# Unit 0 put in another order, index lists fetched one at a time, and one of nine tables gathered instead of looked up in units 3, 5 and 7

## What is computed

```
e = stack([tbl_f[ids[:, f]] for f in range(26)], axis=1)        # 2048 x 26 x 128
combined = concatenate([dense[:, None, :], e], axis=1)          # 2048 x 27 x 128
inter = einsum('bfd,bgd->bfg', combined, combined)              # 27 x 27 for each sample
z = concatenate([dense, inter[:, iu0, iu1]], axis=1)            # 128 + 351
h = concatenate([z, dense], axis=1)                             # 607
h = maximum(h @ W_top1 + b_top1, 0)                             # 512
h = maximum(h @ W_top2 + b_top2, 0)                             # 256
y = h @ W_top3                                                  # 1
```

## Time and profile before

| | |
|---|---|
| median of 3 runs | 402.04 us (401.98 to 402.32) |
| the profiled execution: its time | 402.14 us |
| its span in the trace | 400.4 us |
| PE / PEld / DVE / ACT / POOL busy | 376.2 / 369.1 / 275.1 / 190.2 / 261.3 us |
| granted TensorE clock, mean | 0.991 of full speed |

### The profile page before, as it was taken

How to read it: one execution, slowest core, us unless ns; L and a number is a source line. 1 busy time by engine, 2 the same in 40 slices (tenths; PEclk the granted TensorE clock), 3 DMA queues, 4 the chain that set the end, 5 groups by cost and what they waited for, 6 DMA issues and landing times.

```text
span 400.4 us, 7798 instructions
## 1 busy us (share of the span) xinstructions
PE 376.2 (94%) x3136; PEld 369.1 (92%) x3136; DVE 275.1 (69%) x278; ACT 190.2 (48%) x427; POOL 261.3 (65%) x281
## 2 busy tenths in 40 slices
PE   1998599699999999999999999999999999999996
PEld 1887498599999999999999999999999999999996
DVE  5679582997878486866687486867687486862451
ACT  3475344436642465325642465326643465426643
POOL 7777465777777757776677757776677757774000
PEclk9999799999999999999999999999999999999999
DMA  6944522233324323322324233332323333321000
GB/s 244 383 135 112 186 76 63 52 104 79 87 59 101 81 72 88 79 82 70 90 54 109 74 79 87 80 80 71 90 60 101 78 80 79 81 55 39 2 2 1
DMA packets 18059, 35.49 MB, mean 89 GB/s; under 512 B 5628, under 2 KB 7292, under 8 KB 18024
## 3 DMA queue, kind: packets, MB, share of 16 engines
q0 software_dynamic: 8704, 17.84, 17.9%
q1 hardware_dynamic: 9224, 17.15, 14.2%
q10 hardware_dynamic: 96, 0.00, 0.0%
HBM read 34.97 MB, written 0.01 MB: 87 GB/s over the span
## 4 chain that ended last, share of the span: by engine, by line
PE 92%; DVE 3%; issue 1%; ACT 1%; DMA 1%; SPq 0%; DVEq 0%
PE l_ps L351 31%; PE g_ps L381 28%; PE t_ps L360 7%; PE l_ps L343 6%; PE h_ps L393 5%; PE h_ps L394 5%; PE h_ps L395 5%; PE h_ps L440 2%; PE t_ps L389 1%; DMA hot_idx<-in_hot_ids 1%; DVE onehot L569 1%; DVE zf L599 1%; ACT xT L720 1%; PE g_ps L393 0%; DVE zg L592 0%
## 5 line engine op out<-in xcount | busy, mean ns | idle before, releaser
L317 POOL DMA_INDIRECT emb<-in_tbl,idx x272 | 259.2, 953 | 104.7 <-issue 69.8
L569 DVE TENSOR_TENSOR onehot<-hot_idx,rows_ps 128x2048 fp32r<-128x2048 int32 x72 | 162.4, 2283 | 10.3 <-DMA hot_idx<-in_hot_ids 6.2
L381 PE MATMUL g_ps<-xT 128*123 128x108 f32 x1024 | 118.4, 273 | 5.5 <-DVE hot_low L579 4.7
L381 PEld LDWEIGHTS g_ps<-xT 128*123 128x123 f32 x1024 | 115.3, 190 | 6.0 <-issue 5.9
L351 PE MATMUL l_ps<-onehot,hot_low 128*128 128x256 f32 x528 | 76.5, 287 | 3.2 <-DVE onehot L569 1.8
L351 PE MATMUL l_ps<-onehot,hot_high 128*128 128x256 f32 x528 | 74.1, 283 | 0.0
L740 ACT COPY zg<-g_ps 27x216 f32<-27x216 f32 x160 | 52.8, 330 | 44.8 <-PE g_ps L381 43.7
L351 PEld LDWEIGHTS l_ps<-onehot,hot_low 128*128 128x128 f32 x528 | 67.5, 191 | 4.2 <-ACT xT L720 2.2
L351 PEld LDWEIGHTS l_ps<-onehot,hot_high 128*128 128x128 f32 x528 | 68.1, 192 | 0.0
L720 ACT COPY xT<-l_ps 128x512 f32<-128x512 f32 (+1 forms) x40 | 25.0, 624 | 80.2 <-PE l_ps L351 72.6
L592 DVE COPY zg<-g_ps 27x216 f32<-27x216 f32 x96 | 36.9, 384 | 34.6 <-PE g_ps L381 33.0
(11 more groups left out here) (64 smaller groups left out, 301.2 us busy)
## 6 DMA issues: line engine op xcount, KB each, us to landing
hot_idx<-in_hot_ids SPq DMA_DIRECT2D x36, 256.0 KB, 3.5
stage<-in_hot_tables SPq DMA_DIRECT2D x9, 512.0 KB, 10.2
emb<-in_tbl,idx POOLq DMA_INDIRECT x272, 2.7
dT<-in_dense_t SPq DMA_DIRECT2D x8, 128.0 KB, 2.1
wz<-in_W_pairs SPq DMA_DIRECT2D x1, 512.0 KB
w2s<-in_W_top SPq DMA_DIRECT2D x1, 512.0 KB, 6.6
wz<-in_W_dense SPq DMA_DIRECT2D x1, 256.0 KB
wd<-in_W_dense SPq DMA_DIRECT2D x1, 256.0 KB
```

Of the source, the lines that this page charges most:

```text
L317: pool.indirect_dma_start(emb[:, t % 2, n, :], None, tables[COLD[n]][:, :], bass.IndirectOffsetOnAxis(ap=idx[:, t, n:n + 1], axis=0)).then ...
L381: last = pe.matmul(g_ps[c % 2][0:TALL, i, 0:WIDE], four.rearrange("d s f -> d (s f)")[:, 0:TALL], four[:, :, 0:FEATS], start=True, stop=True)
L569: dve.tensor_tensor(onehot[n % ONEHOTS][:], here, rows, ALU.is_equal).then_inc(onehot_ready, 1)
```

## The change

Three things are changed.

- **Unit 0.** Only three tables (0, 1, 2) are looked up uncut, in place of six; tables 3 to 8 are cut first, in that order, and 0 to 2 last. The programs of PE, DVE and ACT for unit 0 are written in another order to go with it. `one_hot(1, 1)` and `one_hot(1, 2)` move behind the first and the fourth `copy_gram` of tile 0.
- **Lists.** A list is fetched alone (256 ids, 128 KB when spread) in place of a pair (256 KB), into one of three places; list n waits until `onehot` n-3 was made. In unit 0 the lists 3 to 7 stand between the tables on SP, so that tables 4 to 8 queue behind those waits. The fetch of dense features for a unit stands behind its fifth list.
- **Units 3, 5 and 7** (`LEAN`). Table 2, the first hot one, isn't looked up there; POOL gathers its rows as an 18th cold table. Those units have 8 lookups and 36 gathers; the others 9 and 34. `keep_pace` lets POOL begin one step earlier in those units.

```
+LEAN = (3, 5, 7)
-    WHOLE = 6
-    SPLITS = (0, 6, 1) + tuple(range(7, NH)) + (2, 3, 4, 5)
+    WHOLE = 3
+    SPLITS = tuple(range(WHOLE, NH)) + tuple(range(WHOLE))
...
+    FIELDS = COLD + HOT[0:1]
+    def looked(u):
+        return range(1 if u in LEAN else 0, NH)
+    def gathers(u):
+        return NF - len(looked(u))
...
-            def load_indices(i):
-                if i >= 2:
-                    sp.wait_ge(onehot_ready, 2 * i - 2)
+            def load_indices(n):
+                if n >= LISTS:
+                    sp.wait_ge(onehot_ready, n - LISTS + 1)
...
             load_indices(1)
-            for h in range(1, NH):
+            load_indices(2)
+            for h in range(1, 4):
+                load_table(h)
+            for h in range(4, NH):
+                load_indices(h - 1)
                 load_table(h)
             load_dense(0)
...
-                u, m = t // 2, NC * (t % 2) + n
+                u = t // 2
+                m = gathers(u) * (t % 2) + n
...
-                    k = m // 2
-                    if k < 2 * CHUNKS:
-                        pool.wait_ge(gram_done, 2 * CHUNKS * (u - 1) + k + 1)
+                    k = m // 2 + 1 - (u in LEAN)
+                    if k <= 2 * CHUNKS:
+                        pool.wait_ge(gram_done, 2 * CHUNKS * (u - 1) + k)
...
                 layer(u - 1, 1)
-                for h in range(8, NH):
-                    look_up(u, h)
+                for i in range(8, len(looked(u))):
+                    look_up(u, i)
                 turn(odd, 0)
                 layer(u - 1, 2)
...
-            for h in range(4):
+            for h in range(5):
                 one_hot(0, h)
...
+            cut_tables(0, 2)
+            for h in range(5, NH):
                 one_hot(0, h)
-            cut_tables(NH - 4, NH)
+                cut_tables(h - 3, h - 2)
+            cut_tables(NH - 3, NH)
             one_hot(1, 0)
```

More of the change, by code:

```diff
@@ L56, in dlrm_tower, with pairs, lookups, hot_outs @@
     LAYERS = M1 + M2 + 1
-    PAIRS = (NH + 1) // 2
-    ROW_PAIRS = UNITS * NH // 2
-    WHOLE = 6
-    SPLITS = (0, 6, 1) + tuple(range(7, NH)) + (2, 3, 4, 5)
-    assert D == P and sorted(SPLITS) == list(range(NH))
-    RUNS = 5
-    ENDS = [-(-NC * r // RUNS) for r in range(RUNS + 1)]
-    COLD_RUNS = [list(range(a, b)) for a, b in zip(ENDS, ENDS[1:])]
-    assert max(len(run) for run in COLD_RUNS) <= 4
+    FIELDS = COLD + HOT[0:1]
+    def looked(u):
+        return range(1 if u in LEAN else 0, NH)
+    def pairs(u):
+        return (len(looked(u)) + 1) // 2
+    def lookups(u):
+        return sum(len(looked(v)) for v in range(u))
+    def hot_outs(u):
+        return sum(pairs(v) for v in range(u))
+    LOOKUPS = lookups(UNITS)
+    WHOLE = 3
+    SPLITS = tuple(range(WHOLE, NH)) + tuple(range(WHOLE))
+    assert D == P
+    RUNS = 5
+    def gathers(u):
+        return NF - len(looked(u))
+    def cold_run(u, r):
+        run = range(-(-gathers(u) * r // RUNS), -(-gathers(u) * (r + 1) // RUNS))
+        assert len(run) <= 4
+        return run
+    def rows_gathered(t, r):
+        return sum(len(cold_run(v, r)) for v in range(t // 2 + 1))
     ROWS = 32
@@ L82, in dlrm_tower @@
     ONEHOTS = 3
+    LISTS = 3
     def fills(u):
@@ L111, in dlrm_tower @@
         dT = sb("dT", [P, UNIT])
-        emb = sb("emb", [P, 2, NC, D])
+        emb = sb("emb", [P, 2, NC + 1, D])
         xT = sb("xT", [P, 2, P, ROWS])
@@ L154, in dlrm_tower @@
         idx_landed = sem("idx_landed")
-        hot_idx_landed = [sem(f"hot_idx_landed{a}") for a in range(2)]
+        hot_idx_landed = [sem(f"hot_idx_landed{a}") for a in range(LISTS)]
         dense_landed = sem("dense_landed")
@@ L273, in _ @@
             sp.dma_start(small_s[:], small).then_inc(small_landed, 16)
[L274 to L280, removed]
+            load_indices(NH - 1)
+            for u in range(1, UNITS):
+                for i in range(len(looked(u))):
+                    load_indices(lookups(u) + i)
+                    if u == 1 and i == 2:
+                        load_weights()
+                    if i == 4:
+                        load_dense(u)
             sp.wait_ge(y_copied, UNITS)
@@ L331, in begin, with look_up @@
                 return t_ps
[L333 to L338, removed]
+            def look_up(u, i):
+                n, h = lookups(u) + i, looked(u)[i]
+                if i % 2 == 0 and n:
+                    pe.wait_ge(hot_out, hot_outs(u) + i // 2)
+                out = l_ps[:, i % 2, :]
+                picks = onehot[n % ONEHOTS]
                 if u == 0 and h < WHOLE:
@@ L486, in first_unit @@
                 look_up(0, 4)
+                look_up(0, 5)
                 turn(0, 2)
-                look_up(0, 5)
                 look_up(0, 6)
                 turn(0, 3)
-                for h in range(7, NH):
-                    look_up(0, h)
+                look_up(0, 7)
                 turn(0, 4)
+                look_up(0, 8)
                 gram(0, 0)
@@ L663, in _ @@
                     cut_h(u - 1, 0)
-                    for h in range(8, NH):
-                        one_hot(u, h)
+                    for i in range(8, len(looked(u))):
+                        one_hot(u, i)
                     cut_h(u - 1, 1)
@@ L865, in _ @@
                 layer(u - 1, 1)
-                for c in range(4, PAIRS):
+                for c in range(4, pairs(u)):
                     copy_hot(u, c)
```

95 lines of the change are left out of this document (44 added, 51 removed).

## The result

| | before | changed |
|---|---|---|
| median | 402.01 us (401.88 to 402.32, 4 runs) | 390.63 us (389.85 to 391.70, 4 runs) |
| profiled execution: time, span | 402.14, 400.4 us | 391.70, 390.0 us |
| ratio | | 0.9718 [0.9690, 0.9745] |

The four runs of the changed kernel fall into pairs: 389.85 and 390.11 with a mean clock of 0.999, 391.15 and 391.70 with 0.995 and 0.994.

The account below looks back on a forecast made before the run. PE was taken as the bound, busy 376.2 of 400.4 us. Unit 0's 5.1 us and the lean units' 3.06 made 8.2 off 402.14, giving 394.0, with nothing for the clock; range 391.0 to 397.5.

Parts of the forecast that it names:

- Unit 0 up to the first gram: Unit 0, followed in the new order: first gram at 42.4 in place of 47.49, 5.1 us earlier.
- the tables come in time: Unit 0: tables 7 and 8, issued at about 17 and 20.5, wanted at 26 and 30.5; 5 us to landing is covered.
- Behind the first gram: After unit 0's first gram: POOL and DVE follow PE as now; no gain or loss counted.
- The clock: Around the first gram: half clock costs about 2.1 us before and the same after, so nothing won or lost.
- the patchy stretch: PE from 35.4 to 42.4 in unit 0: works only about 2.4 us, so the clock falls there too.
- the bound for lookup 8: Unit 0, worse case: half clock already in lookup 8, 1.9 us longer, 0.6 of it not hidden by the last cut.
- over a third: Unit 0 ahead of the first gram: share of the stretch that is gaps, argued against the clock staying up.
- the clock stays up: Rival for unit 0: clock does not fall, a further 2.1 us won, 391.9 us; chance 0.22.
- The lean units: Units 3, 5 and 7: 1.70 us less PE work, 0.68 given back; 1.02 us won each, 3.06 in all.
- the wait for ACT: Lean units, ahead of layer(2, 2) in unit 3: PE waits for ACT's read of the bank, giving back 0.68 us.
- POOL: Lean units: two extra gathers, 36 at 1.25 us, are hidden at no cost, with 4.1 us to spare.
- Lists in the units: SP's single lists: landing taken as 3.5 us against 4.56 us for two one-hots; 1 us over, no cost.

Follow-up runs that it names:

- e2: Kernel before with lists fetched one at a time into three places, between the tables on the queue; unit 0 in old order, no lean units: 401.75 us, ratio 0.9994.
- g2: Changed kernel with lists 3 to 7 queued behind all nine tables: 399.29 us, ratio 0.9921.
- r5: Changed kernel with one_hot(1, 1) and one_hot(1, 2) put back where the kernel before has them: 392.60 us, ratio 0.9770.
- e4: Kernel before with 40 more identity transposes filling PE's 4.65 us wait ahead of the first gram: 402.28 us, ratio 1.0004.
- g1: Kernel before with only the two one-hots of unit 1 moved as in the change, no filled wait: ratio 0.9979.
- r6: Kernel before with 40 identity transposes in PE's wait ahead of the first gram and unit 1's two one-hots moved as in the change: ratio 0.9941.
- r7: Changed kernel with the lean units' eighth lookup moved from ahead of turn(even, 4) to behind layer(u-1, 1), its ACT copy likewise: 388.04 us, ratio 0.9649.
- r8: Changed kernel with all units 2 to 7 lean instead of 3, 5 and 7: 391.99 us, ratio 0.9751.

## Why the prediction was right and wrong

- **Unit 0 up to the first gram:** right. 5.1 us forecast, 5.6 in the trace, and the chain of one-hots and cuts was followed step by step. That the tables come in time was right too. The runs added that order and queue only work together: e2 gives nothing, and g2 gives 3 us, of which the lean units are 2.8.
- **Behind the first gram:** this step failed. The prediction said "Behind the first gram POOL and DVE follow PE as now" and gave the two moved one-hots no price. They are worth 2 us in the changed kernel (r5 against it, 392.6 and 390.6, and 8.34 us from the first gram to the fourth against 6.39), and only because the first gram runs at full clock there: in the kernel before they give 0.8 alone and 2.4 with the clock kept up.
- **The clock:** "so nothing is won or lost" failed with it. It took 2.1 us for the slow first gram from two durations, as if the path ran over PE there. In the trace of the kernel before it ran over DVE: at full clock the stretch to the fourth gram took the same 8.3 us (e4). So the slow clock cost nothing in that execution, and with DVE out of the way it does cost (8.39 us from the first gram to the fourth in g1, 6.55 with the clock kept up in r6); after the change it would have, but it rose ahead of the first gram. That it fell in the patchy stretch was right, and so was the bound for lookup 8 (1.9 us longer, 0.6 not hidden; 1.8 and about 0.6 in the trace). The stretch was idler than "over a third": by the prediction's own figures 4.6 of 7.0 us are gaps. The rival "the clock stays up", at 391.9, comes nearest to the 391.70 of the profiled execution, by luck: it won its 2.1 us from the clock alone, and e4 shows that the clock alone wins nothing.
- **The lean units:** right, 0.96 for 1.02 each, the wait for ACT in its place. r7 shows that nothing else held the unit up: with a lookup back in the gap it takes 43.20, 1.72 less than 44.92, where the sum had 1.70 before the wait.
- **POOL:** right that it hides the two gathers, in three units with one between, and right in size. 4.1 us to spare were forecast for unit 3. In the changed kernel's trace its last gather starts at 178.64, lands some 2.6 us later, and PE wants it at 185.10: 3.9. In r8 less is to spare, because the lean units begin at unit 2, when POOL has less of a stock: the last gather of unit 2 starts at 133.46 and is wanted at 138.45, 2.4 to spare by the same sum; in unit 3 it is 1.1, and in unit 4 the last turn is 0.2 late.
- **Lists in the units:** right; a pair lands after 3.5 us, a list of half the size after 3.3, so half the bytes save only 0.2 us, and to take 3.5 for both was near. DVE waits for none behind unit 0. The page of the changed kernel:

```profile
hot_idx<-in_hot_ids SPq DMA_DIRECT2D x69, 128.0 KB, 3.3
```

- **The range** ended at 391.0, since the moved one-hots were put at nothing without a bound. The profiled execution, 391.70, is 2.3 us below the 394.0: 2.0 won behind the first gram and 0.5 ahead of it, less 0.2 in the lean units. The median is another 1.1 below, which is spread of the executions that the sum has no term for.

## What to carry to other kernels

A slow duration in a trace can't be priced until the wait that ends last is shown to hang on it; ask of each such stretch who else is as late, since two things that cover each other show little when one of them is mended, and all when both are. Moving work out from between two pieces of a resource's round trip (here PE, ACT's reading of one bank, PE again) lays bare the trip; leave some independent work there. A second order and a second queue may each be worthless alone.

## What was unexpected of the hardware

- The start of the kernel varies: the first two lookups took 8.57 to 9.96 us in the traces of kernels that are alike there (8.57 in r6, 9.90 in the kernel before, 9.96 in r7), and PE began them at 7.45 (g2) to 8.75 (g1). It goes through to the first gram: they end at 18.37 in the kernel before and at 16.69 in e2, 1.68 us apart, and the first gram starts at 47.49 and 45.82, 1.67 apart.
- Two chips ran the kernel before in 476 us in place of 402. In the traces from there a gather (951 ns), a one-hot (2283) and ACT's copies take what they take elsewhere, several engines stand still at once for something unnamed, and every kernel that stands on the changed one was slower than the kernel before. The changed kernel itself wasn't run there.
